# Graph layer: one-hots of one width, summed parts on TensorE, a second-layer product in two pieces, and a new order of the step

## Chip, cores and metric

One Trainium2 chip, one core of it. The metric is the device time of one execution in microseconds (us); three executions of the kernel before took 808.5, 809.54 and 809.83 us, median 809.54.

## What is computed

A graph network layer over 3125 nodes of 32 values (8 scalars, 8 vectors of 3) and 53125 edges, sorted by destination. For every edge:

```
r = edge_vec / |edge_vec|;  xs, xd = x[src], x[dst]
s1 = 16 scalars, v1 = 16 vectors of xs and xd;  vdot1 = v1 . r
w  = relu(emb @ w11) @ w12 ;  s_t, v_t = contractions of s1, vdot1, v1 with w     (first layer)
w2 = relu(emb @ w21) @ w22 ;  scal, gates, vecs = contractions of s_t, v_t with w2 (second layer)
edge_out = [tanh(scal), vecs * tanh(gates)] * norm
out = layernorm(x + segment_sum(edge_out, dst))
```

## The kernel before

The edges go in 104 blocks (`NB`) of 512 (`BE`), each of four tiles of 128. Block m flows through five in-order instruction lists; there is no planner. Each engine's list is written out by hand as a loop over `STEPS`, and in step i it handles block i of one stage, block i+3 of another, and so on; semaphores tie the lists together. What comes after what on each engine is the text of these loops, at the end of each engine's function.

- **GpSimd** gathers the source rows of block i+5 (four indirect DMAs, L337), and in `directions` forms for block i+3 the products of the vectors with the direction (`along`, L379), of the scalars with it (L380), and sums `along` over the three directions in two additions (L383, L385).
- **Destination rows.** Sorted destinations lie in a window of 42 nodes (`WIN`). x is split into three bf16 parts, stored in DRAM as three planes; `load_window` brings the three windows in as 126 rows. VectorE makes the one-hot, 4 x 126 wide (L588), TensorE transposes it (`turn_one_hot`, L831), ScalarE copies it (`copy_oht`, L451), TensorE multiplies it with the window (`rows`, L891, four matmuls over 126 rows, so the three parts add up in one product), and ScalarE copies the rows (`copy_rows`, L476) beside the sources (`copy_sources`, L469).
- **First layer.** TensorE turns the features (`turn_features`, L839), ScalarE copies them (`copy_f`, L457), `first_layer` (L917) writes g to PSUM banks 0 to 3, `hidden` (L909, L910) makes both hidden layers, ScalarE applies relu (L494, L500). VectorE multiplies all four banks with the hidden layer (`products`, L686, 128 x 2048), `sum_1` (L850) sums to v. v is copied as three bf16 parts, each followed by a subtraction on TensorE (`part_of_v`, L488; `less_part`, L857).
- **Second layer.** `repeat` (L879) spreads the parts of v over banks 0 to 3 again by four full products of 128 x 512, VectorE multiplies all four banks with the second hidden layer in one instruction (`products2`, L714), `sum_2` (L863) sums, ScalarE copies (`copy_u`, L463), `turn` (L901) transposes to bank 7, which v uses too. `gates` (L724 to L734) is five VectorE instructions: m1, m4, m2, m5, gsc. tanh is ScalarE's (L445), `outputs` (L704, L707) weights and multiplies, `over_nodes` (L871) sums the edges of a node with the one-hot, `accumulate` (L697) adds to `acc` at a base read from SBUF into a register (L692).
- The embeddings are split into three bf16 parts and stored in DRAM for 12 blocks at a time: ScalarE L510, GpSimd L357 and L360.

The order of a step (block in brackets) before:

```
VectorE: products(i) accumulate(i-4) gates(i-3): m1 m4 m2 m5 gsc  products2(i-1) outputs(i-3) one_hot(i+5)
TensorE: repeat(i-1) turn_one_hot(i+4) sum_1(i) rows(i+3) hidden(i+1) less(i,0) first_layer(i+1) less(i,1)
         over_nodes(i-3) sum_2(i-1) turn_features(i+2) turn(i-2)
ScalarE: copy_oht(i+4) one-hot(i-3) sources(i+3) tanh(i-3) v(i,0) hidden_1(i+1) v(i,1) hidden_2(i+1) rows(i+3)
         v(i,2) copy_u(i-1) copy_f(i+2)
```

Waits that tie them: `first_layer(m)` waits for `z_done` of block m-2, `repeat(k)` for `p_done` of block k+1, `turn(k)` for all three copies of v of block k+2 and for `e_free` of block k-1.

## Time and profile before

| | |
|---|---|
| median of 3 executions | 809.54 us |
| profiled execution, its time | 807.87 us |
| its span | 806.0 us |
| VectorE busy | 739.8 us, 92% |
| TensorE busy | 707.5 us, 88% |
| GpSimd busy | 626.8 us, 78% |
| ScalarE busy | 551.1 us, 68% |
| mean granted TensorE clock | 0.993 of full speed |

The span is that of the instructions on the core; 1.9 us of the execution lie around it. A busy share tells how long an engine had an instruction in flight; instructions overlap at their ends, so spacing from start to start is the finer measure. The rows of the timeline give start, length, engine, line, operation, what is written and read with its size, how many instructions are merged in the row, and in brackets idle time of the engine before it with what ended it.

### The profile page before, as it was taken

Reading aid. Unit: us, or ns where it says so; the run is one execution under the profiler, and the core shown is the slowest. Engines: PE = TensorE matmul, PEld = TensorE weight load, DVE = VectorE, ACT = ScalarE, POOL = GpSimd, SP = SyncE. Lnnn points to the kernel's source line nnn. Section 1 sums busy time; section 2 is a strip of 40 time slices with the busy share of each in tenths; the row PEclk is TensorE's granted clock in tenths of the full one; section 3 lists DMA queues with packets and bytes.
Section 4 is the critical chain, followed back from the end, with each engine's and each line's share of the span. In section 5 each row is a group of like instructions: output and inputs, shape, how many; then the busy total and the mean of one; then the engine's idle time right before and its main releaser. Section 6 shows DMA issues by size and latency. Waiting matters only on the chain.

```text
span 806.0 us, 19013 instructions
## 1 busy us (share of the span) xinstructions
PE 707.5 (88%) x5819; PEld 292.3 (36%) x5922; DVE 739.8 (92%) x1217; ACT 551.1 (68%) x1279; POOL 626.8 (78%) x863
## 2 busy tenths in 40 slices
PE   1687999999999999999999999899999998999974
PEld 1432333333333333333333333333333333333322
DVE  8689999999999999999999999999999999999884
ACT  2367667777777777777776777777777767777642
POOL 8788888788888888888888888888888888888300
PEclk9899999999999999999999999999999999999998
DMA  3321211111111111211112111111111111111000
GB/s 102 89 65 19 44 26 37 24 42 27 38 26 41 24 26 39 43 24 25 36 25 44 26 38 23 42 27 37 27 41 23 26 34 36 26 23 26 12 1 20
DMA packets 44030, 27.24 MB, mean 34 GB/s; under 512 B 22012, under 2 KB 42509, under 8 KB 43930
## 3 DMA queue, kind: packets, MB, share of 16 engines
q1 hardware_dynamic: 29681, 18.24, 8.5%
q0 software_dynamic: 13312, 6.84, 5.7%
q10 hardware_dynamic: 937, 0.93, 0.4%
q8 instruction: 50, 0.82, 0.4%
q14 instruction: 50, 0.41, 0.2%
HBM read 21.77 MB, written 4.20 MB: 32 GB/s over the span
## 4 chain that ended last, share of the span: by engine, by line
DVE 31%; issue 29%; PE 26%; ACT 10%; DVEq 3%; ACTq 0%; POOL 0%; POOLq 0%
PE ps L917 12%; DVE z_s L714 11%; PE ps L879 7%; DVE p_s L686 6%; ACT v_s L488 5%; PE ps L857 3%; ACT ohs L483 3%; DVEq L692 3%; DVE acc L697 2%; DVE m L724 2%; PE ps L831 2%; DVE oh L588 2%; DVE m L729 2%; ACT fe L469 2%; DVE gsc L734 2%
## 5 line engine op out<-in xcount | busy, mean ns | idle before, releaser
L337 POOL DMA_INDIRECT xs<-in_xp,src_i x416 | 435.6, 1047 | 110.1 <-issue 79.3
L686 DVE TENSOR_TENSOR p_s<-ps,h 128x2048 f32<-128x2048 f32 x104 | 238.2, 2291 | 41.0 <-PE ps L917 36.3
L714 DVE TENSOR_TENSOR z_s<-ps,h 128x2048 f32<-128x2048 f32 x104 | 237.8, 2286 | 2.5 <-PE ps L879 2.3
L488 ACT CAST v_s<-ps 128x512 bf16<-128x512 f32 x312 | 181.9, 583 | 48.4 <-PE ps L857 39.1
L451 ACT COPY oht<-ps 126x512 bf16<-126x512 bf16 x104 | 61.0, 586 | 115.8 <-PE ps L831 110.6
L917 PE MATMUL ps<-f,w_f 32*128 32x512 f32 x832 | 119.6, 641 | 17.1 <-DVE z_s L714 7.5
L850 PE MATMUL ps<-p_s,sum_m 128*32 128x512 f32 x832 | 110.8, 604 | 4.9 <-DVE m L731 3.6
L879 PE MATMUL ps<-v_s,rep_m 128*128 128x512 bf16 x315 | 85.3, 379 | 26.4 <-DVE acc L697 22.7
L863 PE MATMUL ps<-z_s,w_z 128*32 128x512 f32 x832 | 108.1, 591 | 0.0
L463 ACT COPY u<-ps 128x512 f32<-128x512 f32 x104 | 61.1, 588 | 56.7 <-PE ps L863 56.7
L857 PE MATMUL ps<-v_s,less 128*128 128x512 bf16 x206 | 80.3, 390 | 13.6 <-ACT v_s L488 3.6
L839 PEld LDWEIGHTS ps<-ident,fe 128*128 128x128 f32 x416 | 44.1, 142 | 87.8 <-issue 87.0
L857 PEld LDWEIGHTS ps<-v_s,less 128*128 128x128 bf16 x208 | 19.9, 96 | 143.1 <-ACT v_s L488 141.5
L588 DVE TENSOR_TENSOR oh<-rank,place 128x504 bf16<-128x504 bf16 x104 | 70.5, 679 | 0.0
L839 PE MATMUL ps<-ident,fe 128*128 128x128 f32 x416 | 69.1, 289 | 1.3 <-ACT fe L476 1.3
L379 POOL TENSOR_TENSOR along<-fe,r 128x192 f32<-128x192 f32 x104 | 55.1, 530 | 12.9 <-ACT fe L476 6.0
L494 ACT ACTIVATE h<-ps 128x512 f32<-128x512 f32 x104 | 63.2, 608 | 0.8 <-PE ps L909 0.8
L457 ACT COPY f<-ps 128x512 f32<-128x512 f32 x104 | 60.9, 586 | 3.6 <-PE ps L839 3.6
L901 PE MATMUL ps<-ident,u 128*128 128x128 f32 x416 | 62.6, 273 | 0.0
L500 ACT ACTIVATE h<-ps 128x512 f32<-128x512 f32 x104 | 62.6, 602 | 0.0
L831 PE MATMUL ps<-ident_h,oh 128*126 128x128 bf16 x416 | 41.8, 224 | 19.8 <-DVE oh L588 19.8
L380 POOL TENSOR_TENSOR fe<-fe,r 128x192 f32<-128x192 f32 x104 | 55.4, 532 | 0.0
(116 smaller groups left out, 904.8 us busy)
## 6 DMA issues: line engine op xcount, KB each, us to landing
emb<-e_dram SPq DMA_DIRECT2D x312, 30.0 KB
xs<-in_xp,src_i POOLq DMA_INDIRECT x416
e_dram<-e_part SPq DMA_DIRECT2D x7, 360.0 KB
e_in<-in_emb SPq DMA_DIRECT2D x8, 240.0 KB
window<-x_dram SPq DMA_DIRECT2D x104, 7.9 KB
x_dram<-eo_all SPq DMA_DIRECT2D x3, 195.3 KB
eo_all<-in_vec_t SPq DMA_DIRECT2D x1, 528.0 KB, 4.1
xt_n<-in_xt SPq DMA_DIRECT2D x1, 400.0 KB, 3.7
```

What stands on the lines that cost most here:

```text
L337: nc.gpsimd.indirect_dma_start(xs_r[n][:, t, :], None, xp, bass.IndirectOffsetOnAxis(src_i[:, m * T + t:m * T + t + 1], axis=0)).then_inc( ...
L488: nc.scalar.copy(v_s[:], v_ps).then_inc(v_step, 1)
L494: nc.scalar.activation(h1_r[m % 2][:], h1_ps, ACT.Relu, scale=1.0 / math.sqrt(10.0)).then_inc(h1_ready, 1)
L588: nc.vector.tensor_tensor(oh_r[m % OH][:], rank[:].unsqueeze(1).to_broadcast([128, T, WK]), place[:, T * m:T * m + T].unsqueeze(2).to_broa ...
L686: nc.vector.tensor_tensor(p_s[:], ps[:, 0:4, :], h1_r[m % 2][:].unsqueeze(1).to_broadcast([128, 4, BE]), ALU.mult).then_inc(p_done, 1)
L714: nc.vector.tensor_tensor(z_s[:], ps[:, 0:4, :], h2_r[k % 3][:].unsqueeze(1).to_broadcast([128, 4, BE]), ALU.mult).then_inc(z_done, 1)
L839: last = nc.tensor.transpose(f_ps[:, TE * t:TE * t + TE], fe_r[m % 2][:, t].rearrange("p g c -> p (g c)"), ident[:])
L850: last = nc.tensor.matmul(v_ps[32 * g:32 * g + 32], sum_m[:].rearrange("p n c -> p (n c)"), p_s[:, g, :], start=True, stop=True)
L857: nc.tensor.matmul(v_ps, less[n][:], v_s[:], start=False, stop=True, skip_group_check=True).then_inc(s1_step, 1)
L863: last = nc.tensor.matmul(s2_ps[32 * g:32 * g + 32], w_z[:, min(g, 1), :], z_s[:, g, :], start=True, stop=True)
L879: last = nc.tensor.matmul(ps[:, g, :], rep_m[:, g].rearrange("p j c -> p (j c)"), v_s[:], start=True, stop=True)
L917: last = nc.tensor.matmul(ps[:, g, :], w_f[32 * g:32 * g + 32], f_r[m % 2][32 * g:32 * g + 32], start=True, stop=True)
```

## The change

It does these things together.

1. The one-hot is 42 wide and not 126; the window is loaded as 42 rows with the three parts side by side, x being stored in that layout, and `rows` adds the parts by three matmuls a tile, accumulated in PSUM.
2. `products2` becomes two instructions of two banks each; `repeat` still makes four full products, and signals after the second and after the fourth.
3. The two additions over directions leave GpSimd; VectorE does them in one reduce (`sum_along`), with `along` double.
4. `gates` is cut in two, with m2 and gsc behind the second product; `outputs` is cut in two and moved by a step; `over_nodes` and `accumulate` move by a step or two; the register load of the base stands behind `products2`.
5. `hidden` is cut in two, and the lists of TensorE and ScalarE are put in a new order.
6. In the set-up: one-hots 0 to 2 are made first, one store of x for three, the first embeddings are split earlier and loaded by ScalarE's queue, and `late_constants` move into step 0. The last `turn` uses bank 0, and the loops run two steps longer.

The order of a step after:

```
VectorE: products(i) gates(i-3): m1 m4 m5  products2(i-1) in two  base(i-5) weighting(i-4) accumulate(i-5)
         gate_sums(i-3): m2 gsc  outputs(i-4) sum_along(i+2) one_hot(i+5)
TensorE: repeat(i-1) sum_1(i) over_nodes(i-5) rows(i+3) hidden_1(i+1) less(i,0) first_layer(i+1) turn_one_hot(i+4)
         less(i,1) sum_2(i-1) turn(i-2) turn_features(i+2) hidden_2(i+1)
ScalarE: v(i,0) hidden_1(i+1) v(i,1) rows(i+3) sources(i+3) copy_oht(i+4) v(i,2) tanh(i-3) copy_u(i-1) copy_f(i+2)
         one-hot(i-4) hidden_2(i+1)
```

The core of the diff:

```diff
-        window_r = [sb(f"window{n}", [WK, D], BF16) for n in range(3)]
-        oh_r = [sb(f"oh{n}", [128, T, WK], BF16) for n in range(OH)]
+        window_r = [sb(f"window{n}", [WIN, PARTS, D], BF16) for n in range(3)]
+        oh_r = [sb(f"oh{n}", [128, T, WIN], BF16) for n in range(OH)]
...
-        STEPS = range(-5, NB + 4)
+        STEPS = range(-5, NB + 6)
...
                 if m == CA:
                     pool.wait_ge(r4_ready, 2)
-                nc.gpsimd.tensor_tensor(along[:], fe[:, :, 1:4, 0:16], r, ALU.mult).then_inc(fe_step, 1)
+                nc.gpsimd.tensor_tensor(along_r[m % 2][:], fe[:, :, 1:4, 0:16], r, ALU.mult)
                 nc.gpsimd.tensor_tensor(fe[:, :, 1:4, 16:32], fe[:, :, 0:1, 0:16].to_broadcast([128, T, 3, 16]), r,
                                         ALU.mult).then_inc(directed, 1)
-                pool.wait_ge(fe_step, 2 * m + 1)
-                nc.gpsimd.tensor_tensor(pair[:], along[:, :, 0, :], along[:, :, 1, :], ALU.add).then_inc(fe_step, 1)
-                pool.wait_ge(fe_step, 2 * m + 2)
-                nc.gpsimd.tensor_tensor(fe[:, :, 0, 16:32], pair[:], along[:, :, 2, :], ALU.add).then_inc(along_done, 1)
...
+            copy_oht(0)
+            act.wait_ge(emb_zeroed, 1)
+            act.wait_ge(e_stored, 16)
+            for first in (0, 32, 64):
+                act.dma_start(emb_r[0][first:first + PARTS * HID], e_dram[:, 0:HID, :]).then_inc(emb_loaded[0], 16)
...
+            def late_constants():
+                link(nc.vector.tensor_scalar(w_z[:], w_z[:], c2, None, ALU.mult))
+                nc.vector.tensor_scalar(w_z[:, 0, 16:24], w_z[:, 0, 16:24], SQRT3, None, ALU.mult).then_inc(weights_ready, 1)
+                nc.vector.tensor_copy(iota[:], iota_i[:]).then_inc(consts_ready, 1)
+                link(nc.vector.tensor_reduce(strip_sum[:], ident[:].rearrange("p (g c) -> p c g", g=4), AX.X, ALU.add))
+                nc.vector.tensor_scalar(centre[:], strip_sum[:], -1.0 / D, None, ALU.add).then_inc(consts_ready, 1)
...
+            def sum_along(m):
+                dve.wait_ge(directed, m + 1)
+                nc.vector.tensor_reduce(fe_r[m % 2][:, :, 0, 16:32], along_r[m % 2][:].rearrange("p t k u -> p t u k"), AX.X, ALU.add
+                                        ).then_inc(along_done, 1)
...
             def products2(k):
-                dve.wait_ge(rep_done, k + 1)
                 dve.wait_ge(h2_ready, k + 1)
-                nc.vector.tensor_tensor(z_s[:], ps[:, 0:4, :], h2_r[k % 3][:].unsqueeze(1).to_broadcast([128, 4, BE]),
-                                        ALU.mult).then_inc(z_done, 1)
+                for n in range(2):
+                    dve.wait_ge(rep_done, 2 * k + n + 1)
+                    ins = nc.vector.tensor_tensor(z_s[:, 2 * n:2 * n + 2], ps[:, 2 * n:2 * n + 2, :],
+                                                  h2_r[k % 3][:].unsqueeze(1).to_broadcast([128, 2, BE]), ALU.mult)
+                ins.then_inc(z_done, 1)
...
             def repeat(k):
...
                 for g in range(4):
                     last = nc.tensor.matmul(ps[:, g, :], rep_m[:, g].rearrange("p j c -> p (j c)"), v_s[:],
                                             start=True, stop=True)
-                last.then_inc(rep_done, 1)
+                    if g % 2 == 1:
+                        last.then_inc(rep_done, 1)
...
                 for t in range(T):
-                    last = nc.tensor.matmul(rows_ps[:, t, :], oht_r[m % 2][:, TE * t:TE * t + TE], window_r[m % 3][:],
-                                            start=True, stop=True)
+                    for n in range(PARTS):
+                        last = nc.tensor.matmul(rows_ps[:, t, :], oht_r[m % 2][:, TE * t:TE * t + TE],
+                                                window_r[m % 3][:, n, :], start=(n == 0), stop=(n == PARTS - 1))
```

## Rows read from the trace of the kernel before

**Rows 1.** Timeline, VectorE: first and last of the 104 first-layer products (start, length, instruction)
```profile
35.20 2.29 DVE L686 TENSOR_TENSOR p_s<-ps,h 128x2048 f32<-128x2048 f32 x1 [5.88 <-PE ps L917]
...
773.24 2.29 DVE L686 TENSOR_TENSOR p_s<-ps,h 128x2048 f32<-128x2048 f32 x1 [0.88 <-PE ps L917]
```

**Rows 2.** Timeline, VectorE, one undisturbed step
```profile
402.29 2.29 DVE L686 TENSOR_TENSOR p_s<-ps,h 128x2048 f32<-128x2048 f32 x1 [0.33 <-PE ps L917]
404.50 0.19 DVE L697 TENSOR_TENSOR acc<-acc,ps 128x42 f32 x1
404.69 0.43 DVE L724 TENSOR_TENSOR m<-ps,r 128x256 f32<-128x256 f32 x1
405.03 0.25 DVE L726 TENSOR_TENSOR m<-ps,r 128x96 f32<-128x96 f32 x1
405.19 0.28 DVE L729 TENSOR_TENSOR m<-m 128x128 f32<-128x128 f32 x1
...
405.56 0.23 DVE L734 TENSOR_TENSOR gsc<-m 128x64 f32<-128x64 f32 x1
405.72 2.29 DVE L714 TENSOR_TENSOR z_s<-ps,h 128x2048 f32<-128x2048 f32 x1
407.93 0.21 DVE L704 TENSOR_TENSOR eo_all<-eo_all,wgt_s 128x64 f32<-128x64 f32 x1
408.18 0.29 DVE L707 TENSOR_TENSOR eo_all<-m,eo_all 128x96 f32<-128x96 f32 x1
408.35 0.68 DVE L588 TENSOR_TENSOR oh<-rank,place 128x504 bf16<-128x504 bf16 x1
```

**Rows 3.** Timeline, TensorE, the same step
```profile
402.17 0.39 PE L857 MATMUL ps<-v_s,less 128*128 128x512 bf16 x1
402.49 0.28 PE L871 MATMUL ps<-ohs,eo_all 128*32 128x42 f32 x8
402.59 1.04 PE L863 MATMUL ps<-z_s,w_z 128*32 128x512 f32 x8
403.56 0.65 PE L839 MATMUL ps<-ident,fe 128*128 128x128 f32 x4
404.05 0.60 PE L901 MATMUL ps<-ident,u 128*128 128x128 f32 x4
404.87 0.81 PE L879 MATMUL ps<-v_s,rep_m 128*128 128x512 bf16 x3 [0.22 <-DVE acc L697]
405.52 0.39 PE L831 MATMUL ps<-ident_h,oh 128*126 128x128 bf16 x4
405.84 1.06 PE L850 MATMUL ps<-p_s,sum_m 128*32 128x512 f32 x8
406.84 0.27 PE L891 MATMUL ps<-window,oht 126*128 126x32 bf16 x4
406.95 0.38 PE L909 MATMUL ps<-emb,w_first 96*128 96x512 bf16 x1
...
408.16 1.14 PE L917 MATMUL ps<-f,w_f 32*128 32x512 f32 x8
```

**Rows 4.** Timeline, VectorE in the set-up: a reduce of 192 elements to 64
```profile
7.30 0.35 DVE L602 TENSOR_REDUCE eo_all<-r 128x64 f32<-128x192 f32 x1
```

**Rows 5.** Instructions of L692, the load of a base (ns: least, median, most)
```profile
L692 DVEq TENSOR_LOAD <-bases x104: 298/304/557, 63.6 to 792.9; - x104
```

**Rows 6.** Timeline, a disturbed step: VectorE's m2 and GpSimd's first product
```profile
255.42 0.86 DVE L729 TENSOR_TENSOR m<-m 128x128 f32<-128x128 f32 x1
...
255.60 0.53 POOL L379 TENSOR_TENSOR along<-fe,r 128x192 f32<-128x192 f32 x1
```

**Rows 7.** Timeline, VectorE: the last accumulate
```profile
793.57 0.20 DVE L697 TENSOR_TENSOR acc<-acc,ps 128x42 f32 x1 [1.08 <-PE ps L871]
```

**Rows 8.** Timeline, ScalarE: second hidden layer and the copy of the rows
```profile
408.56 0.60 ACT L500 ACTIVATE h<-ps 128x512 f32<-128x512 f32 x1
409.05 0.27 ACT L476 COPY fe<-ps 128x128 f32<-128x128 f32 x1
```

More of the change, by code:

```diff
@@ L24 @@
 PARTS = 3
-WK = PARTS * WIN
 OH = 10
@@ L100, in program @@
         fe_r = [sb(f"fe{n}", [128, T, 4, 32]) for n in range(2)]
-        along = sb("along", [128, T, 3, 16])
-        pair = sb("pair", [128, T, 16])
+        along_r = [sb(f"along{n}", [128, T, 3, 16]) for n in range(2)]
         f_r = [sb(f"f{n}", [128, BE]) for n in range(2)]
@@ L113, in program @@
         m4 = sb("m4", [128, T, 3, 8])
-        m5 = sb("m5", [128, T, 3, 8])
+        m5_r = [sb(f"m5_{n}", [128, T, 3, 8]) for n in range(2)]
         ohs_r = [sb(f"ohs{n}", [128, T, WIN]) for n in range(2)]
@@ L424, in _ @@
                         if i == -3:
-                            gather(2, 2, T)
+                            gather(2, 1, T)
                         if i == -2:
@@ L746, in _ @@
                     products2(i - 1)
-                if real(i - 3):
-                    outputs(i - 3)
-                if real(i + 5) and i + 5 >= 2:
+                if real(i - 5):
+                    base = base_of(i - 5)
+                if real(i - 4):
+                    gated(i - 4)
+                if real(i - 5):
+                    accumulate(i - 5, base)
+                if real(i - 3):
+                    gate_sums(i - 3)
+                if real(i - 4):
+                    outputs(i - 4)
+                if real(i + 2):
+                    sum_along(i + 2)
+                if real(i + 5) and i + 5 >= 4:
                     one_hot(i + 5)
+                if i == 0:
+                    late_constants()
                 for step, at_step in enumerate((0, 1, 3, 4, 5, 6, 7, 8)):
@@ L927, in keep_warm @@
                 for _ in range(n):
-                    nc.tensor.matmul(ps[:, 0, 0:128], ident[:], ident[:], start=True, stop=True)
+                    nc.tensor.matmul(ps[:, 1, 0:128], ident[:], ident[:], start=True, stop=True)
             def nodes_themselves():
@@ L939, in _ @@
                     repeat(i - 1)
-                if real(i + 4):
-                    turn_one_hot(i + 4)
+                if real(i):
+                    sum_1(i)
+                if real(i - 5):
+                    over_nodes(i - 5)
+                if real(i + 3):
+                    rows(i + 3)
                 if i == -4:
```

175 lines of the change are left out of this document (91 added, 84 removed).

## The prediction, made before the changed kernel ran

> **What bounds the kernel now.** I read the table of busy shares first: VectorE and TensorE are both near nine tenths busy, so neither share decides anything. The spacing of the 104 first-layer products does: from the first at 35.20 to the last at 773.24 [rows 1] lie 103 intervals, 738.0 us, 7.17 us each. The run of one step in order of time (VectorE in [rows 2], TensorE in [rows 3]) shows 7.06 us in an undisturbed step, and that number can be rebuilt. Banks 0 to 3 hold both the first layer's product g and the repeated v, so a step is one closed round through them: VectorE's first product 2.29, 0.05 to the first weight load of the repeat, four repeat matmuls 1.04, 0.04 to the second product (405.68 to 405.72), 2.29, then 0.15 until the first layer starts (408.01 to 408.16), 1.14 for it, 0.06 back to VectorE. The sum is 7.06. The four repeat matmuls are 0.65 + 0.38 + 0.01: the trace holds three of them, 0.81 long, each 0.38, so they follow at 0.215, and the fourth, at 404.66, has no record. In the last step the second half of VectorE's list is nearly empty, it idles 0.88 before the product [rows 1], and the spacing is still 7.06: the round through the banks is the limit, with VectorE (0.33 idle, [rows 2]) and TensorE (0.22 idle, [rows 3]) close behind. 7.06 times 103 is 727; the other 11 us are disturbed steps, read below.
>
> **The round through the banks, after.** The second product comes in two pieces; the first waits for two repeat matmuls (0.215 + 0.38 = 0.60) and not for four. From [rows 2], 2048 elements space the next instruction by 2.21, 96 elements by 0.16: 1.05 ns an element and 0.06 fixed. A piece of 1024 is 1.14, both 2.28, and 0.08 until the last one ends. Round: 2.29 + 0.05 + 0.60 + 0.04 + 2.36 + 0.15 + 1.14 + 0.06 = 6.69. This is the gain of the split, 0.37, bought with 0.06 of VectorE's time.
>
> A rule speaks against the split. The Trainium skill (VectorE: DVE Perf Modes, "The DRAIN you can't avoid") says that the next operation does not start until the pipe has emptied, and tells authors to keep the count of operations small. By that the second piece would cost 0.08 more and the step 0.08 more. The same page allows that an operation which isn't held starts earlier, and this trace agrees with that: 404.50 follows 402.29 by 2.21 while the first lasts 2.29.
>
> **VectorE's own list, after.** Spacing by spacing: first product 2.21; m1 0.34; m4 0.28 (its 0.25 and 0.03, since m5 now stands right behind it and waits for it; between the weighting and the output, 407.93 + 0.21 to 408.18, such a wait is 0.04); m5 0.16; two pieces 2.28; weighting 0.16 (64 elements, as gsc); accumulate 0.19; m2 0.31 (0.28 and the wait, as gsc stands right behind it now); gsc 0.16; output 0.17; the sum over directions, new here, 0.28; the one-hot 0.25. Sum 6.79. The sum over directions reads 192 elements and writes 64; the set-up has a reduce of that very form, 0.35 long [rows 4], less the 0.08 overlap. Here its inner step is 16 elements and not one, which no row prices; bounds are 0.28 and, as a stride might cost, 0.40; I take 0.28, the row's. The one-hot shrinks from 504 to 168 elements: 0.68 - 336 x 1.05 ns = 0.33 long, 0.25 spacing. The register load of the base is 0.30 and some register work, about 0.65 in all [rows 5]; today it lies under the first product, then under the second piece (1.14). If that cover were too short, it would add up to 0.2.
>
> **TensorE's list, after.** The part that matters runs from the end of the second product to the next repeat: 0.15 to the start; first layer 1.07 (1.14, and the next form of matmul starts 0.07 before the modelled end, as 402.59 + 1.04 to 403.56 shows); transposing the one-hot, moved here, 4 x 0.057 = 0.23 (0.39 for four of 0.22); second subtraction 0.32 (402.17 to 402.49, with the change of form in it); second layer's sum 0.97; turning u, now ahead, 0.49; turning features 4 x 0.11 = 0.44; the second hidden product, moved here, 0.22; two repeat matmuls 0.60; 0.04; both pieces 2.36 [rows 2, 3]. Sum 6.89. The product over nodes (0.10) leaves this part. Turning u also waits for ScalarE's third copy of v, now behind the one-hot's copy: its end comes 2.71 us after the second product, the turn would start at 2.74 anyway. So a tie, good for 0.02. The rows' product gets 12 matmuls for 4. The four took 0.11 (406.84 to 406.95), so eight more are 0.2, in a stretch that waits for the first copy of v and then for the second product; cost nothing, and 0.1 a step if that cover is gone. Stationary tiles have 42 rows and not 126; at 32 columns no row says that this is slower or faster.
>
> The largest of 6.69, 6.79 and 6.89 sets the step: TensorE's list, by 0.1. I add 0.02 for the tie: **6.91 a step**. GpSimd loses two additions a step and gains only freedom. ScalarE does the same work in another order; with its hidden-layer copy last it isn't in the round.
>
> **Sum.** Steps: 103 x 6.91 = 712, and 5 us for disturbed steps. Of today's 11, some 4 fall in the first nine steps (late set-up arithmetic on VectorE, GpSimd's backlog), and most of the rest where GpSimd's backlog from splitting the embeddings reaches VectorE's m2 [rows 6]: 0.86 for 0.28. In the new order GpSimd has two instructions less, so it catches up, but late constants come into step 0. 717 against 738: -21. Start: the first product no longer waits for a one-hot copy that stood ahead of the hidden layer, the late constants (about 2.5 us of VectorE) move into the loop, and the first embeddings are split and loaded earlier; but ScalarE's queue now issues these loads. First product at about 31.7 for 35.2: -3.5, bounds 0 and -7. End: from the last first-layer product to the last accumulate it is 20.3 us [rows 1, 7]; the last turn there stands behind a product over nodes that waits for a tanh; that goes, the split gives 0.4, and two more steps with register loads that nothing covers (0.65 each) come: -2, bounds +1 and -4. Sum -26.5 against the profiled execution's 807.9 gives 781.4. The median of the runs is 1.7 above that execution; 783, and I say 784, since a hand-made schedule leaves out small waits.
>
> **Rivals.**
> *A, the forecast, 0.58.* 6.86 to 6.98 a step, 778 to 790; with start and end at their bounds 774 to 795.
> *B, given back in part, 0.22.* The stride of the reduce (+0.1), the register load coming out from its cover, or the rows' matmuls make VectorE's or TensorE's list 7.0 to 7.08. For it: lists at 6.79 and 6.89 leave so little spare that each small miss is felt in full. Time: 7.03 x 103 = 724, + 5 is 729, 9 under today's, and 5.5 for start and end: 795; the case spans 792 to 800.
> *C, slower: the one-hot meets GpSimd's first product, 0.17.* In [rows 6] m2 started 0.18 before GpSimd's 192-element product, would have ended 0.10 into it, and ended 0.15 behind it instead. So two-input operations of both engines in SBUF can shut each other out. Today GpSimd's products lie beside VectorE's first product, which reads PSUM. After, GpSimd waits for ScalarE's copy of the sources. Counted from the repeat: the sum starts at 0.95 (1.18 less the one-hot's turn), ScalarE's row copy 3.21 behind it less the 0.49 of the hidden copy that leaves [rows 3, 8], 0.2 more for the rows' matmuls, sources and hand-over 0.6: about 4.4 to 4.5. The one-hot starts at 0.64 + 2.28 + 1.27 = 4.19, or 4.4 with the bounds above, and lasts 0.33. They meet within a tenth. If GpSimd wins, the one-hot ends 0.15 behind its 0.53, the next first product starts near 4.97, and the round is 4.97 + 2.34 = 7.31 in every step, as both sides hang on the same repeat: 103 x 7.31 = 753, +15 - 5.5, about 819. It decides from the point at which over three quarters of the steps are met; in a third of them it gives 796. Against it: m2 was caught by a GpSimd that came straight from a gather, while here it comes from a wait and may take its input later.
> The Trainium skill (SBUF — State Buffer, "Who interferes with whom") has this as a lock: a two-input VectorE operation in SBUF and a GpSimd operation that reads SBUF exclude each other, and the first to start keeps it. By its letter the one-hot, which starts first, wins, and the time is A's; it also holds the new reduce free of this. The trace agrees in part: m2 started first and lost.
> *D, the split does not act, 0.03.* If the first piece starts only behind all four repeat matmuls, TensorE's sum is 6.89 + 0.44 = 7.33: about 821.
>
> **How the numbers follow.** The time is A's. 774 to 815 takes in A with the bounds of start and end, B, and the greater part of C; A's own range is 774 to 795. A measurement of this kernel tells some 0.2%, 1.6 us, from no change. Faster: A, nearly all of B: 0.77. Same: the edges of B and C, 0.03. Slower: C and D, 0.20.
>
> **What would show it.** Spacing of first-layer products 6.9 in the middle; the first piece starting about 0.7 behind the end of the first product, and before the fourth repeat matmul ends; VectorE's idle time ahead of the first product under 0.1; the repeat's first weight load no longer waiting for VectorE but following the hidden product; rows' matmuls x12 in about 0.3; the one-hot at 0.33. Wrong: a one-hot of 0.7 or more beside GpSimd's product (C), m2, gsc or the reduce longer than booked or a gap ahead of the weighting (B), the first piece at 1.1 behind the first product (D).

## The result, and where the time went

The changed kernel takes 803.93 us (median of 4 executions, 803.35 to 804.40) against 809.23 us (4 executions) for the kernel before beside it: a ratio of 0.9935, 95% interval [0.9917, 0.9952]. That is 5.3 us, where 25 were forecast. The direction was right and the time lies in the range, but four fifths of the gain did not come.

Page of after: the span, the chain that ended last by engine, then by line.

```profile
span 802.0 us, 20705 instructions
...
PE 72%; DVE 18%; issue 6%; DVEq 2%; DMA 1%; ACT 1%; POOL 0%; SPq 0%; POOLq 0%
PE ps L960 14%; PE ps L896 12%; DVE z_s L729 11%; PE ps L914 8%; PE ps L940 7%; PE ps L880 7%; PE ps L868 5%; PE ps L887 4%; PE ps L860 4%; PE ps L928 3%; PE ps L953 3%; DVE p_s L690 3%; PE ps L947 2%; DVEq L696 1%; PE ps L971 1%
```

TensorE holds 72% of the chain (26% before); that its list would set the step was the forecast. Timeline of after, VectorE: first and last first-layer product, last accumulate (these answer to [rows 1, 7]).

```profile
36.73 2.29 DVE L690 TENSOR_TENSOR p_s<-ps,h 128x2048 f32<-128x2048 f32 x1 [2.88 <-PE ps L960]
...
767.38 2.29 DVE L690 TENSOR_TENSOR p_s<-ps,h 128x2048 f32<-128x2048 f32 x1 [0.44 <-PE ps L960]
...
789.54 0.20 DVE L703 TENSOR_TENSOR acc<-acc,ps 128x42 f32 x1 [1.01 <-PE ps L906]
```

These times cut the difference of the two profiled executions, 4.0 us, into parts:

| us | before | after | difference | forecast |
|---|---|---|---|---|
| start, to the first product | 35.20 | 36.73 | +1.5 | -3.5 |
| 103 steps | 738.0 | 730.65 | -7.4 | -21 |
| of these: an undisturbed step, x 103 | 7.06 | 7.075 | +1.5 | -15 |
| of these: disturbed steps | 10.9 | 1.9 | -8.9 | -6 |
| last product to last accumulate | 20.3 | 22.2 | +1.8 | -2 |
| what follows | 12.4 | 12.5 | 0 | 0 |

So the whole gain is that steps are no longer disturbed; the undisturbed step, on which the forecast rested, did not get shorter at all. Of the 103 spacings, before had 7.06 in the middle with one of 7.7 to 7.9, mostly beside one of 7.18, each time the embeddings of 12 more blocks were split; after, all from the eleventh to the third from the end lie within 0.03 of 7.075. What disturbance is left, 2.5, lies in the first ten, and the last two are 0.3 shorter each. Which edit took the disturbance away no run isolates: GpSimd lost its two additions, and m2 moved behind the second product, both in the same change.

Timeline of after, VectorE, one step (answers to [rows 2]).

```profile
400.02 2.29 DVE L690 TENSOR_TENSOR p_s<-ps,h 128x2048 f32<-128x2048 f32 x1
...
402.87 0.25 DVE L746 TENSOR_TENSOR m<-m,ps 128x96 f32<-128x96 f32 x1
403.40 2.36 DVE L729 TENSOR_TENSOR z_s<-ps,h 128x1024 f32<-128x1024 f32 x2 [0.28 <-PE ps L914]
...
405.91 0.29 DVE L750 TENSOR_TENSOR m<-m 128x128 f32<-128x128 f32 x1
...
406.55 0.36 DVE L722 TENSOR_REDUCE fe<-along 128x64 f32<-128x192 f32 x1
406.83 0.32 DVE L587 TENSOR_TENSOR oh<-rank,place 128x168 bf16<-128x168 bf16 x1
407.10 2.29 DVE L690 TENSOR_TENSOR p_s<-ps,h 128x2048 f32<-128x2048 f32 x1
```

The sizes booked for VectorE are there: the reduce at 0.36 in spacing 0.28, the one-hot at 0.32, the two pieces 2.36 together. Its list has one idle time, 0.28 ahead of the pieces, and that is TensorE's repeat. The first piece starts 1.09 behind the end of the first product (402.31 to 403.40). The prediction wanted 0.7 and named 1.1 as the sign of rival D; the sign was badly set, since 0.7 holds only where the round through the banks is the limit, and here the repeat itself starts 0.39 behind that product, at the end of TensorE's list. Timeline of after, TensorE, one step (answers to [rows 3]); the bound stretch runs from the first layer at 405.90 round to the repeat.

```profile
400.55 1.06 PE L896 MATMUL ps<-z_s,w_z 128*32 128x512 f32 x8
401.55 0.66 PE L940 MATMUL ps<-ident,u 128*128 128x128 f32 x4
402.04 0.60 PE L868 MATMUL ps<-ident,fe 128*128 128x128 f32 x4
402.48 0.38 PE L953 MATMUL ps<-emb,w_first 96*128 96x512 bf16 x1
402.70 1.03 PE L914 MATMUL ps<-v_s,rep_m 128*128 128x512 bf16 x4
...
405.90 1.14 PE L960 MATMUL ps<-f,w_f 32*128 32x512 f32 x8 [0.39 <-issue]
406.97 0.40 PE L860 MATMUL ps<-ident_h,oh 128*42 128x128 bf16 x4
407.31 0.39 PE L887 MATMUL ps<-v_s,less 128*128 128x512 bf16 x1
407.63 1.06 PE L896 MATMUL ps<-z_s,w_z 128*32 128x512 f32 x8
```

Start to start: 0.14 from the end of the second piece (405.76) to 405.90; first layer 1.07; transposing the one-hot **0.34**; subtraction 0.32; second layer's sum 1.00; turning u 0.49; features 0.44; hidden 0.22; two repeats 0.59; then **0.11** to the first piece, and 2.36 for both. The sum is 7.08. The forecast had the same list with 0.23 and 0.04 at the two marked places and came to 6.89 (6.91 with its tie). Two small terms, 0.18 together, are 18 us over 103 steps. In the record the first piece starts when two repeat matmuls are done and before the fourth ends, so the split acts.

### The profile page after: what moved, and what is told of

The parts are those of the page before. It is cut to its first block, busy times and chain, and to the rows that moved or that the text cites. A ratio compares the mean times of both kernels' runs of the same rounds, so it can differ in the third digit from the quotient of the medians.

```text
span 802.0 us, 20705 instructions
## 1 busy us (share of the span) xinstructions
PE 719.7 (90%) x6667; PEld 338.6 (42%) x6770; DVE 732.6 (91%) x1425; ACT 553.8 (69%) x1279; POOL 531.4 (66%) x655
## 4 chain that ended last, share of the span: by engine, by line
PE 72%; DVE 18%; issue 6%; DVEq 2%; DMA 1%; ACT 1%; POOL 0%; SPq 0%; POOLq 0%
PE ps L960 14%; PE ps L896 12%; DVE z_s L729 11%; PE ps L914 8%; PE ps L940 7%; PE ps L880 7%; PE ps L868 5%; PE ps L887 4%; PE ps L860 4%; PE ps L928 3%; PE ps L953 3%; DVE p_s L690 3%; PE ps L947 2%; DVEq L696 1%; PE ps L971 1%
## 5 line engine op out<-in xcount | busy, mean ns | idle before, releaser
L335 POOL DMA_INDIRECT xs<-in_xp,src_i x416 | 403.6, 970 | 111.7 <-issue 97.6
L729 DVE TENSOR_TENSOR z_s<-ps,h 128x1024 f32<-128x1024 f32 x208 | 245.0, 1220 | 27.6 <-PE ps L914 26.7
L914 PE MATMUL ps<-v_s,rep_m 128*128 128x512 bf16 x415 | 106.7, 379 | 3.7 <-DVE p_s L690 3.7
L446 ACT COPY oht<-ps 42x512 bf16<-42x512 bf16 x104 | 60.3, 580 | 55.3 <-PE ps L860 55.2
L940 PEld LDWEIGHTS ps<-ident,u 128*128 128x128 f32 x416 | 43.5, 140 | 86.4 <-issue 86.4
L868 PE MATMUL ps<-ident,fe 128*128 128x128 f32 x416 | 63.0, 274 | 0.1
L914 PEld LDWEIGHTS ps<-v_s,rep_m 128*128 128x128 bf16 x416 | 39.8, 98 | 43.7 <-DVE p_s L690 6.6
L860 PEld LDWEIGHTS ps<-ident_h,oh 128*42 128x42 bf16 x416 | 24.3, 101 | 78.1 <-issue 75.7
L906 PEld LDWEIGHTS ps<-ohs,eo_all 128*32 128x32 f32 x832 | 28.5, 109 | 58.1 <-issue 57.7
L928 PE MATMUL ps<-window,oht 42*128 42x32 bf16 x1248 | 48.1, 174 | 5.0 <-DMA window<-x_dram 3.5
```

The costliest lines, as they stand in the source:

```text
L335: nc.gpsimd.indirect_dma_start(xs_r[n][:, t, :], None, xp, bass.IndirectOffsetOnAxis(src_i[:, m * T + t:m * T + t + 1], axis=0)).then_inc( ...
L729: ins = nc.vector.tensor_tensor(z_s[:, 2 * n:2 * n + 2], ps[:, 2 * n:2 * n + 2, :], h2_r[k % 3][:].unsqueeze(1).to_broadcast([128, 2, BE]) ...
L868: last = nc.tensor.transpose(f_ps[:, TE * t:TE * t + TE], fe_r[m % 2][:, t].rearrange("p g c -> p (g c)"), ident[:])
L914: last = nc.tensor.matmul(ps[:, g, :], rep_m[:, g].rearrange("p j c -> p (j c)"), v_s[:], start=True, stop=True)
L928: last = nc.tensor.matmul(rows_ps[:, t, :], oht_r[m % 2][:, TE * t:TE * t + TE], window_r[m % 3][:, n, :], start=(n == 0), stop=(n == PART ...
L940: last = nc.tensor.transpose(ps[:, bank, TE * t:TE * t + TE], u_r[k % 2][:, TE * t:TE * t + TE], ident[:])
```

## Experiments

Steps are given as the median spacing of first-layer products, since it is free of start and end. A single time without an interval is one execution. The start is a coarser measure: over the nine runs that leave the stores and the clock-keeping matmuls of the start alone, after among them, the first product comes between 35.80 and 38.16.

### The two terms of the step

**Transposes 126 columns wide.** Only the transposes of the one-hot get their old form back; they also turn columns that nobody reads.

```diff
-last = nc.tensor.transpose(oht_ps[:, TE*t:TE*t+TE], oh_r[m % OH][:, t, :], ident_h[:])
+last = nc.tensor.transpose(oht_wide[:, TE*t:TE*t+TE], oh_w_all[:, m % OH, WIN*t:WIN*t+126], ident_h[:])
```

> The changed kernel, with the one-hot still computed 42 wide but transposed as 126 columns from where each tile starts (84 zero columns stand behind the last one; the rows above 42 of the transpose are never read). Theory T (the step is set by TensorE's list, and the narrow transpose costs it a change of form: the subtraction starts 0.335 us behind the transposes and not 0.23): that spacing goes back to about 0.23, the spacing of first-layer products from 7.075 to 6.97-6.98, the time by about 10 us, to 794. Rival V (VectorE's list sets the step): spacing unchanged at 7.07, TensorE merely waits longer before the repeat. Rival N (narrow operands are slow as such, form plays no part): the transposes themselves would get slower or stay, and no 0.1 appears behind them.

Measured: 799.9 us, step 7.033, where 6.97 to 6.98 was expected. The subtraction followed the transposes by 0.28, for 0.34 and for the 0.23 expected, though they turn three times as many columns. So it is not the number of columns that costs but their form. Of the 0.06 gained there 0.042 arrived at the step; why, the run after the next shows.

**One wait ahead of the pieces.** The first piece waited for two semaphores, the second hidden layer and the repeat. The wait for the hidden layer goes to the head of VectorE's step, where it has long been met.

```diff
 def products2(k):
-    dve.wait_ge(h2_ready, k + 1)
     for n in range(2):
...
+if real(i - 1):
+    dve.wait_ge(h2_ready, i)
 if real(i):
     products(i)
```

> The changed kernel, with VectorE's wait for the second hidden layer moved from in front of the first half product to in front of the first-layer product, so that the half product has only the wait for the repeat. Theory T: the half product today starts 0.107 us behind the second repeat matmul where the undivided one before started 0.04 behind the fourth; the second semaphore in front of it costs the difference. Then that gap falls to about 0.04, the spacing from 7.075 to 7.00-7.01, the time by about 7 us, to 797. Rival (the gap is the way TensorE reports a matmul in mid-stream, nothing to do with the waits): gap stays near 0.107, spacing stays 7.07.

Measured: 797.74 us, step 7.006, as expected, and the piece follows the repeat by 0.04 for 0.107. The start of this run was 0.5 later than after's, so all of the gain is from the steps (723.8 for 730.65).

The number of waits is not what costs. The first-layer product has two waits as well, in before and in after, and follows the matmul that releases it by 0.06; in this run, with a third, it follows by 0.11. Timelines of the last steps, where VectorE is idle ahead of it, after and then this run:

```profile
759.42 1.14 PE L960 MATMUL ps<-f,w_f 32*128 32x512 f32 x8
760.62 2.29 DVE L690 TENSOR_TENSOR p_s<-ps,h 128x2048 f32<-128x2048 f32 x1 [0.20 <-PE ps L960]
...
753.11 1.14 PE L961 MATMUL ps<-f,w_f 32*128 32x512 f32 x8
754.37 2.29 DVE L690 TENSOR_TENSOR p_s<-ps,h 128x2048 f32<-128x2048 f32 x1 [0.25 <-issue]
```

The trace tells the difference. One wait rides on the product, and it is the one written first; the others stand in an instruction of their own ahead of it. In after this is (instructions of L728, ns):

```profile
L728 DVEq EVENT_SEMAPHORE  x104: 21/21/21, 47.2 to 776.2; - x104
```

By its record it waits for the repeat, the semaphore that comes last, 0.04 behind the matmul, and the piece starts 0.065 behind its start. In before `products2` waits for the repeat first and for the hidden layer second, so the separate instruction holds the wait that has long been met, 0.19 ahead of the product, and the product follows the repeat by 0.04. The change turned the two lines round. What the run shows, then, is that a wait that comes last costs 0.06 to 0.07 more when it is not the one on the product; the same holds for this run's first-layer product. There it is hidden in the middle, but not in the last two steps, which stayed at 6.75 for 6.76. No run puts the two lines back in their old order, which by this reading would do.

**66 columns.** The window of 42 rounded up past 64, to see whether width or form counts.

```diff
-... oh_w_all[:, m % OH, WIN*t:WIN*t+126]
+... oh_w_all[:, m % OH, WIN*t:WIN*t+66]
```

> As the run with the wide transpose, but with 66 columns and not 126. If the 0.1 us is a change of form at 64 columns, 66 columns are as good as 126: spacing 6.97-6.98. If the cost falls gradually with the width, the subtraction follows the transposes at about 0.29 and the spacing is about 7.03.

Measured: 796.73 us, step 7.002. Timelines of this run, TensorE and then ScalarE:

```profile
408.94 0.41 PE L864 MATMUL ps<-ident_h,oh 128*66 128x128 bf16 x4
409.18 0.38 PE L891 MATMUL ps<-v_s,less 128*128 128x512 bf16 x1
409.49 1.07 PE L900 MATMUL ps<-z_s,w_z 128*32 128x512 f32 x8
410.54 0.63 PE L944 MATMUL ps<-ident,u 128*128 128x128 f32 x4
...
409.38 0.58 ACT L449 COPY oht<-ps 42x512 bf16<-42x512 bf16 x1 [0.43 <-PE ps L864]
409.87 0.58 ACT L486 CAST v_s<-ps 128x512 bf16<-128x512 f32 x1
```

The subtraction follows by 0.24. With 42 columns it was 0.34, with 66 it is 0.24, with 126 it was 0.28: between 42 and 66 something changes that costs 0.10, and beyond it more columns cost a little. In the records of the single matmuls (medians of 85 steps, start to start) it all stands behind the last transpose: the subtraction follows that by 0.152 at 42 columns, by 0.056 at 66 and 0.058 at 126, while the first transpose follows the first layer by 0.518 at every width. In before the sum, 32 columns wide, followed the last transpose of 126 by 0.151. The Trainium skill (TensorEngine Tiling (Array Packing), "Key Properties") says that a change of tiling mode drains TensorE, and its table has a dimension of up to 64 as a narrower tile; by it the 42 columns are a mode of their own between the first layer and the subtraction, one change more than at 66. The trace agrees, with 0.10 for it; the page has no figure. The second thing in these rows is the next limit: turning u follows the sum by 1.05 for 1.00, because it waits for ScalarE's third copy of v, which ends at 410.45 behind the copy of the one-hot. The features then follow the turn by 0.46 for 0.49, so that 0.02 of the 0.10 is lost: the tie of the forecast, which only shows now.

**Both edits, with 126 columns** (the wide transposes and the wait moved).

> Both edits together. Theory T, if TensorE's list sets the step all along: 7.075 - 0.105 - 0.07 = 6.90 us a step, about 786 us in all. Rival V (VectorE's list takes over soon): the sum of VectorE's spacings in the changed kernel is 6.71, so it would not; if it does nonetheless, the two gains do not add and the spacing stops at 6.95 or more.

Measured: 792.94 us, ratio to before 0.9774 [0.9758, 0.9791], step 6.963. The two gains add up (7.075 - 0.042 - 0.069 = 6.964). Of the 0.06 over the expected 6.90, 0.04 is the width (0.28 for 0.24) and 0.02 would be the order of ScalarE's copies, which the next run tried.

**The third copy of v ahead of the one-hot's copy**, with 66 columns and one wait.

```diff
+if real(i):
+    part_of_v(i, 2)
 if real(i + 4) and i + 4 >= 1:
     copy_oht(i + 4)
-if real(i):
-    part_of_v(i, 2)
```

> The changed kernel with the one-hot turned 66 columns wide, one wait ahead of VectorE's products, and ScalarE's third copy of v ahead of its copy of the one-hot. The run of 66 columns took the change of form away (sum at .24 behind the transposes) but its turn of u then stood behind the third copy of v, .09 later than TensorE's list wants it. Theory (TensorE's list is the limit, the third copy of v next in line): 7.075 - .07 for the second wait - .10 for the transposes = 6.90 to 6.91 a step, about 786. Rival (VectorE's own list, 6.71 and its waits, or the second wait and the copy of v are no separate terms): the step stays at 6.93 to 6.96, as in the run of both edits with 126 columns.

Measured: 789.49 us, step 6.909. Timeline of this run, TensorE:

```profile
406.16 0.41 PE L865 MATMUL ps<-ident_h,oh 128*66 128x128 bf16 x4
406.40 0.38 PE L892 MATMUL ps<-v_s,less 128*128 128x512 bf16 x1
406.71 1.06 PE L901 MATMUL ps<-z_s,w_z 128*32 128x512 f32 x8
407.71 0.66 PE L945 MATMUL ps<-ident,u 128*128 128x128 f32 x4
```

Transposes 0.24, turn of u 1.00 behind the sum, and the step is the 6.91 of the forecast (7.075 - 0.073 - 0.069 = 6.933, and 0.024 for the copy). What was missing in the step were these terms and nothing else.

### The split itself

**The new order without the split.**

```diff
-    for n in range(2):
-        dve.wait_ge(rep_done, 2 * k + n + 1)
-        ins = nc.vector.tensor_tensor(z_s[:, 2*n:2*n+2], ...)
+    dve.wait_ge(rep_done, 2 * k + 2)
+    nc.vector.tensor_tensor(z_s[:], ps[:, 0:4, :], ...)
```

> The changed kernel, with the second-layer product of VectorE again in one instruction behind all four repeat matmuls. Theory T (round of TensorE's list, the second product and back): the product starts 0.43 later behind the repeat, less 0.07 for one wait fewer and 0.06 for one instruction fewer: 7.075 + 0.43 - 0.13 = 7.37 us a step, about 835 us: the split is then worth 0.3 a step inside the new order. Rival (the order alone is worth as much, the split is hidden): spacing stays near 7.07.

Measured: 845.26 us, step 7.443. The split is worth 0.37 a step in this order: two repeat matmuls (0.43) less what the second piece adds (0.07). The 0.07 over the expected 7.37 was taken off for one wait fewer, but the product still has both and still follows the repeat by 0.108. The rest of the change without the split is 4% slower than the kernel before. This run also shows what rival C had described. Timelines, VectorE and GpSimd:

```profile
404.99 0.61 DVE L587 TENSOR_TENSOR oh<-rank,place 128x168 bf16<-128x168 bf16 x1
...
404.90 0.51 POOL L377 TENSOR_TENSOR along<-fe,r 128x192 f32<-128x192 f32 x1 [1.50 <-ACT fe L464]
```

Here GpSimd's product starts 0.09 ahead of the one-hot, and the one-hot ends 0.19 behind it, 0.61 long (median of 80: 0.58) for 0.32. It costs the step nothing, since TensorE's list is 7.44 by its own terms. Once in 12 blocks a step of 7.67 comes back here, although GpSimd has no additions. In after the product starts at 407.07, 0.24 behind the one-hot's 406.83, and the one-hot takes 0.317 to 0.328 in all 85 steps of the middle: in these two runs the one-hot is longer only where GpSimd is first. The Trainium skill (SBUF — State Buffer, "Who interferes with whom") says just that, the first to start keeps the shared ports; these two runs agree, [rows 6], where m2 began first and ended last, did not.

**The split alone, in the old order** (the edit of `products2` and the signals of `repeat`, on the kernel before).

> The kernel before, with only the second-layer product divided in two and the repeat signalling twice. Theory (there the product waits for VectorE's own five gate instructions, which end as the fourth repeat matmul does, so an earlier first half finds VectorE busy): the split brings nothing and costs its 0.06 and perhaps a second wait, spacing 7.12-7.19 for 7.06, time 815 to 822. Rival (the repeat was what the product waited for): spacing falls towards 6.8.

Measured: 819.7 us against 810.62, ratio 1.0118 [1.0099, 1.0137]; undisturbed step 7.096, mean in the middle 7.25. VectorE's own gates stood in front of the second product there, so an earlier repeat had nobody waiting, and the second piece was pure cost, 0.04 (at least 0.06 was expected). Each time embeddings were split, two steps of 7.99 came where before mostly had 7.18 and 7.76. Rows by line over 100 to 700 us, the last of the gates, gsc, in this run:

```profile
L736 DVE TENSOR_TENSOR gsc<-m 128x64 f32<-128x64 f32 x82 | 30.6, 373 | 0.0
```

Its mean is 373 ns; in the kernel before it was 268, in after it is 228. So the split and the rest of the change need each other: the split alone costs 1.2%, the rest alone 4%.

### The start

**The store of the embeddings held back until x has landed.** In after the single store of x (586 KB) is issued at 14.85 and the windows that need it are loaded at 23.94; before, at 18.49.

```diff
 act.wait_ge(e_part_ready, PARTS)
+act.wait_ge(x_stored, 32)
 act.dma_start(e_dram...)
```

> The changed kernel, with ScalarE's store of the first embedding parts held until the store of x has landed. Theory S (the start is late since both stores are issued at 14.9 and share the DMA engines, so that x lands 9 us later and the windows are loaded at 23.9 for 18.5): windows are loaded at 19 to 20, embeddings land at about 24, the first first-layer product comes at 32 to 33 for 36.7, time about 4 us less. Rival (the one store of 586 KB needs its 9 us by itself): windows at 23.9 still, embeddings later, the first product at 38 or later.

Measured: 802.92 us, first product 35.91, which is within the spread of runs that leave the start alone. The windows were loaded 1.2 earlier, at 22.74, not 4 to 5: neither the theory nor its rival. The table of windows tells why: with nothing beside it but GpSimd's gathers, the store kept 0.39 of the DMA engines busy, the store of the embeddings behind it 0.87 (window; busy of PE, PEld, DVE, ACT, POOL; clock, DMA share, GB/s).

```profile
19.00:20.00 1.00, 1.00 (x7) 1.00 (x6) 0.90 (x4) 0.00 (x0) 0.96 (x1) 1.00 0.39 130
...
23.00:24.00 1.00, 0.00 (x0) 0.00 (x0) 0.93 (x6) 0.41 (x1) 0.00 (x0) 1.00 0.87 214
```

**No clock-keeping matmuls ahead of the first turn.** Timeline of after, SyncE and TensorE:

```profile
14.85 0.29 SPq L294 DMA_DIRECT2D x_dram<-eo_all  x1
23.94 3.39 SPq L261 DMA_DIRECT2D window<-x_dram  x3
...
26.27 0.47 PE L928 MATMUL ps<-window,oht 42*128 42x32 bf16 x12 [3.49 <-DMA window<-x_dram]
26.67 3.61 PE L971 MATMUL ps<-ident 128*128 128x128 f32 x16
30.21 0.40 PE L860 MATMUL ps<-ident_h,oh 128*42 128x128 bf16 x4
```

TensorE idled 3.49 for the window, the granted clock then read 0.54 (the level of 1.2 GHz for nearly all of 26.6 to 30.3), and the 16 matmuls that are there to keep it up took 3.61 and stood ahead of the second one-hot's turn.

```diff
-if i == -3:
-    keep_warm(8)
```

> The changed kernel without the group of clock-keeping matmuls ahead of the first one-hot's turn (26.7 to 30.3 in the trace of after). Theory: they stand in the path of the start, the first product comes at about 33.5 for 36.7. Rival: the path there is the windows' load and GpSimd's work behind it, and the clock stays at a half into the first steps: first product at 36 to 37, first nine steps longer than 66.4.

Measured: first product 34.26, 2.5 earlier than in after and 1.5 earlier than in the earliest of the nine runs, where the theory had 33.5. The granted clock read 1.00 from 26.6 to 37, but the matmuls do not bear it out: the transposes of a one-hot took 0.61 to 0.62 and the first layer at 32.11 took 2.09, where at full speed they take 0.40 and 1.14. So near the start speed is read from the lengths; the group of 16 at 18.45 in after too took 3.78 under a reading of 1.00. The time is 803.36 all the same, since this run's tail was 23.8 (below).

**The store of x in 112 and 13 partitions.** x lies in 125 partitions of 25 nodes.

```diff
-sp.dma_start(x_dram[0:N, :]..., x_part...).then_inc(x_stored, 16)
+for p0, p1 in ((0, 112), (112, P)):
+    sp.dma_start(x_dram[p0*NT:p1*NT, :]..., x_part[p0:p1]...).then_inc(x_stored, 16)
```

> The changed kernel with its one store of x (125 partitions) cut into one of 112 partitions and one of 13, issued one after the other. Theory: a transfer of 125 partitions keeps only part of the 16 DMA engines busy (share 0.39 at some 130 GB/s while it is alone, as the three stores of before also showed), while the store of the embeddings, 120 partitions in three runs each, shows 0.87; 112 is a multiple of 16 and fills them: the windows are issued at 19 to 20 for 23.94 and the first product comes at 34 for 36.73. Rival (the bytes themselves, both stores together or one queue's rate, are the limit): the windows stay at 22 to 24, first product at 36 to 37.

Measured: 800.19 us, first product 31.87. Table of windows (columns as above), then timelines of SyncE, TensorE and VectorE:

```profile
16.00:17.00 1.00, 0.00 (x0) 0.00 (x0) 0.97 (x3) 0.00 (x0) 0.91 (x1) 1.00 0.94 281
...
20.46 3.12 SPq L261 DMA_DIRECT2D window<-x_dram  x3
...
23.48 2.05 PE L972 MATMUL ps<-ident 128*128 128x128 f32 x16
...
31.87 2.29 DVE L691 TENSOR_TENSOR p_s<-ps,h 128x2048 f32<-128x2048 f32 x1 [0.24 <-PE ps L961]
```

Both stores together now reach 0.94 and 281 GB/s (in after, 0.88 and 225) and are over by 19, where the DMA share falls to 0.13; in after x still moved at 0.29 to 0.39 until 22. The windows are loaded 3.5 earlier. TensorE idles 0.8 ahead of the first of them and not 3.5, and the 16 matmuls behind it run at the upper level: 2.05 for 3.61, and for 3.30 to 3.78 in the ten runs with the single store and this group. 3.5 and 1.6 cover the 4.9 by which the first product is earlier than in after; it is 3.9 earlier than in the earliest of the nine runs. The theory of this run had 34, the prediction 31.7. The Trainium skill (DMA: Bandwidth & Descriptors, "Why a DMA increments its semaphore by 16 and not by 1") says that a transfer uses as many DMA engines as the largest number up to 16 that divides the slowest dimension of both its ends; by it 125 partitions go over 5 engines and 112 over 16. The shares agree in kind, 0.39 with the gathers' own in it and 0.94; how many engines moved it no view here counts.

### The end

**Weighting and gate sums ahead of the base's load in the last steps.**

```diff
-base = base_of(i - 5)
 gated(i - 4)
+gate_sums(i - 3)
+base = base_of(i - 5)
 accumulate(i - 5, base)
-gate_sums(i - 3)
```

> The changed kernel, with the last four steps of VectorE in another order: weighting and the sums of the gates before the base is loaded and the nodes are accumulated. Theory: in the last steps the register load (0.65 us) and the wait for the product over nodes stand in front of m2 and gsc, on which the next tanh hangs; from the last first-layer product to the last accumulate it is 22.2 us for 20.3 before the change, and falls to about 20.5. Rival (the two added steps of products over nodes set the end): stays at 22.

Measured: 803.43 us, last product to last accumulate 22.15: nothing. The load of the base is not in the path of the end as after has it.

**No clock-keeping matmuls in the last steps** (with the edit of the run above). Timeline of after, TensorE, last steps:

```profile
782.89 0.28 PE L906 MATMUL ps<-ohs,eo_all 128*32 128x42 f32 x8
783.11 0.66 PE L940 MATMUL ps<-ident,u 128*128 128x128 f32 x4
783.60 1.95 PE L971 MATMUL ps<-ident 128*128 128x128 f32 x16
785.48 0.28 PE L906 MATMUL ps<-ohs,eo_all 128*32 128x42 f32 x8
785.69 2.05 PE L971 MATMUL ps<-ident 128*128 128x128 f32 x16
```

```diff
-keep_warm(4)
-if i in (NB + 1, NB + 2):
-    keep_warm(8)
-if i == NB + 3:
-    keep_warm(4)
```

> The changed kernel without the matmuls that only keep TensorE's clock up in the last steps, and with the weighting and the gate sums ahead of the base's load there. Theory: those matmuls (groups of 1.16, 1.95, 2.05 and 1.16) stand in TensorE's list between the products over nodes and are in the path of the end: last first-layer product to last accumulate 19.5 to 20 for 22.2. Rival: without them the granted clock falls to a half, the last products and transposes take twice as long, and the tail stays at 22 or grows.

Measured: 801.26 us, last product to last accumulate 19.63 for 22.16. Timeline of this run, TensorE:

```profile
783.70 0.28 PE L910 MATMUL ps<-ohs,eo_all 128*32 128x42 f32 x8 [1.98 <-DVE eo_all L715]
784.61 0.28 PE L910 MATMUL ps<-ohs,eo_all 128*32 128x42 f32 x8 [0.62 <-DVE eo_all L715]
785.89 0.90 PE L1037 MATMUL ps<-acc,centre 128*32 128x400 f32 x4 [1.00 <-DVEq L819]
```

The products over nodes now wait for VectorE and not for TensorE's own filler. Of the 2.5 gained, 1.4 is given back behind: the clock read 0.61 in 786 to 790, where the products of the layer norm stand, and what follows the last accumulate took 13.9 for 12.5.

From the last product to the last accumulate the tail has two lengths in these runs whatever the edit in the steps: 22.15 to 22.23 (after and three runs) and 23.64 to 23.81 (the others with those matmuls). In the two of the longer kind whose windows were read, the clock was 0.62 and 0.63 in 778 to 782, where 16 products of the nodes' own rows stand. What decides it is open; it moves the time of a single execution by 1.6. That is more than the 1.1 that leaving out these matmuls gains in all, so of that run only the 2.5 ahead of the last accumulate is clear of it.

### All together

66 columns, one wait, v's copy first, no clock-keeping matmuls at either place, and the tail's order.

> All of these together: 66 columns, one wait, the third copy of v first, no clock-keeping matmuls at the start of the flow and in the last steps. If each term is its own: 103 x (7.075 - 6.905) = 17.5 off, start 3 off, end 2 off: 803.9 - 22.5 = 781. If start and end give nothing: 786 to 787. If the copy of v gives nothing: 789 to 790.

Measured: 785.82 us (5 executions), ratio to before 0.9723 [0.9708, 0.9737]. Of the 22.5 expected if every term were its own, the steps gave 15.7, the start 2.4 (first product 34.31) and the end 0.4: the tail is 0.9 shorter, and what follows it 0.5 longer. With the store of x in two parts as well:

> The version that joins all edits, with the store of x cut in 112 and 13 partitions as well. If the store is the limit of the start and the clock-keeping matmuls are gone: first product at about 31.5 for 34.31, 783 for 785.8. If not: 785.8.

Measured: 783.39 us (5 executions) against 811.15, ratio **0.9664** [0.9648, 0.9679]. Step 6.909, first product 32.12, tail 21.1 and 13.4 behind it. It beats both kernels. The first product is no earlier than the 31.87 of the run that kept the matmuls at the start. There the transposes of the next one-hots took 0.40 and the features 0.63; here, without the group, they took 0.63 and 1.11. So once the store is quick, leaving the group out is worth nothing that these two runs show.

## Why the prediction was wrong, step by step

- **What bounded the kernel before: half read.** The round through the banks is 7.06, but so is the same round by way of VectorE's accumulate and five gates, which fill the 3.43 from the first product to the second (402.29 to 405.72 in [rows 2]) without a gap. The run with the split alone shows it: the repeat was ready 0.43 earlier and the step did not fall. The prediction left this out; the new order clears it, since accumulate, m2 and gsc stand behind the second product there.
- **What bounds the step after: right.** TensorE's list, then VectorE's, then the round through the banks. In the last steps, where the transposes are gone from TensorE's list, the spacing fell to 6.76: the round of 6.69 with 0.07 for the wait for the repeat.
- **"Transposing the one-hot, moved here, 4 x 0.057 = 0.23": the step that failed first.** It measured 0.34. The forecast took four times the spacing inside a group of transposes, with nothing for the step to the next form, and said of narrow stationary tiles in the rows' product that no row tells; it never asked that of the transposes, which sit in the bound stretch. A row had it: in [rows 3] the sum, of 32 columns, follows four transposes of 126 by 0.32 (405.52 to 405.84) and not by 0.23. Counted over 103 steps this is 11 us. With 66 columns it measured 0.24.
- **"0.04" between the repeat and the first piece: failed, 0.11 measured.** 0.04 came from a product of before that carries the wait for the repeat itself. After, the two waits stand in the other order, and the one for the repeat is in an instruction of its own, 0.065 ahead. 7 us; with the other wait moved away, it measured 0.04.
- **"So a tie, good for 0.02": right, but hidden.** TensorE was late by the terms above, so the third copy of v was no limit in after. When these were gone it was worth 0.024.
- **VectorE's list 6.79: right**, 6.71 measured; reduce, one-hot and pieces within 0.03. Rival B's named causes (stride, register load, the rows' 12 matmuls at 0.4 for four's 0.11, under cover) did not act, although the size of the miss, 7.03 forecast in B and 7.075 measured, is B's and more.
- **The split: right**, 0.37 a step, and rival D is refuted. The rule that spoke against it in the prediction did not act: the second piece starts 1.14 behind the first, which lasts 1.22.
- **Disturbed steps: too timid.** 5 us were left for them, 1.9 are there (2.5 in the first ten steps, less 0.6 for the two short ones at the end); m2 has 0.282 to 0.299 in all the middle for up to 0.862. The one gain that came is thus the one that the prediction argued least, and its cause is not isolated.
- **Rival C: refuted here, its mechanism shown.** In the order without the split GpSimd is first and the one-hot takes 0.58. Counted from the repeat the one-hot started at 4.13 (forecast 4.19 to 4.4) and GpSimd's product at 4.37 (4.4 to 4.5), so the forecast of both held within a tenth at its lower bounds, and the order of the two was as close a call as it said. The times given for C and D, 819 and 821, leave out the 5 us of disturbed steps that A and B have.
- **Start, -3.5: failed, +1.5.** "One store of x for three" was costed at nothing. Three stores were issued from 8.71 on as each part became ready; one store must wait for the last part and then runs over few DMA engines. That held the windows 5.4 later; TensorE idled 3.49 for them and then ran at the lower level. With the store in 112 and 13 partitions the first product is at 31.87. That this is the forecast's 31.7 is partly luck: its own terms for the start were not measured one by one, and it had no store in them.
- **End, -2: failed, +1.8.** The tanh was a wait of before, but in TensorE's list behind it stand clock-keeping matmuls, groups of 8, 16 and 8 before and of 8, 16, 16 and 8 after: the longer loop brought one more group of 16, 2.05. The forecast did not read them. Without them the last accumulate comes 2.5 sooner, but what follows it runs slower and takes 1.4 back.

With the two terms of the step, the store and the filler mended, the kernel lands at 783.4 where the forecast said 784. The step agrees for its reasons (6.909 for 6.91). The rest of the agreement is partly luck: the steps took 2 us less than forecast, the start 0.4 more and the end 3.8 more. The model of the step was sound; two numbers in it had been taken from places of another form, and at the start and the end two things, the single store and the filler matmuls, had been costed at nothing.

## What to carry to other kernels

When a list has no slack, each hand-over in it must be priced from a row of the same form: the same order of waits, the same tile shape before and after. Of several waits ahead of an instruction, write the one that comes last first (read from the traces; no run of its own). A saving in columns that leaves an instruction in a form other than its neighbours' can cost more than it saves; rounding up can be the faster choice. Look at the outermost dimension of every transfer on the path, and at filler matmuls that a re-ordered list leaves in front of real work.

## What was not expected of the hardware

- Four bf16 transposes spaced the next matmul, of 128 columns, by 0.34 at 42 columns, 0.24 at 66, 0.28 at 126; the 0.10 stands behind the last of them, and there is as much from 126 columns to 32.
- Of two semaphore waits ahead of a VectorE product one rides on it and the other is an instruction of its own. A product whose last-coming wait was the separate one started 0.107 behind the matmul that released it, and 0.04 with one wait; the first-layer product, with two waits and the last-coming one on it, 0.058, and 0.114 when a third wait pushed that off.
- A store of 586 KB from 125 partitions moved at 130 GB/s and a DMA share of 0.39, gathers beside it; cut in 112 and 13 it reached 0.94 and 281 GB/s together with the second store.
- A VectorE operation with two inputs in SBUF lasted 0.58 to 0.61 for 0.32 when GpSimd's product had started 0.09 earlier, and was untouched when GpSimd started 0.24 later.
- Matmuls ran at half speed under a granted clock that read 1.00: 2.09 for 1.14 for a first layer and 0.62 for 0.40 for four transposes near the start, in the run without the group of 16.
